# Attention scores in two slots of three PSUM banks instead of three slots of two

## The chip, the core and the metric

One core of a Trainium2 chip runs the whole program. The metric is the device time of one execution in microseconds (us), as the median of the runs. PE is the matrix engine (its weight loads have their own row, PEld), ACT the scalar engine, DVE the vector engine, POOL the GpSimd engine, SP the sync engine that issues most DMAs.

## The reference

```python
x = x + attn(layernorm(x))                       # x: 2 x 2048 x 512
x = x + ffn(layernorm(x))
# attn: q = 4 groups x 8 heads x 16, k and v = 8 heads x 16
scores = einsum('bsqhd,bthd->bqhst', qh, kh) * 16 ** -0.5
probs  = softmax(scores, axis=-1)                # 2 x 4 x 8 x 2048 x 2048
a_dot  = einsum('bqhst,bthd->bsqhd', probs, vh)
sigma_q = elu(q)
a_mem  = sigma_q @ memory / (sigma_q @ memory_norm)
out    = a_dot * (1 - w) + a_mem * w
# ffn: x quantised to fp8 and back, times the fp8 weight times its scale
```

The bulk is the softmax: 2 x 4 x 8 x 2048 x 2048 = 268 million exponentials.

## The kernel before, in words

After a prologue (projections, until about 168 us) the program works through 64 *heads* n = 0 to 63: eight chunks of 512 queries (n // 8), each with eight key heads (n % 8). A head has 64 *strips*; a strip is 128 keys x 512 queries of one query group, one PSUM bank. Four strips (the four query groups) over the same 128 keys make a key *tile*, and a head has 16 tiles. The last head (63) is done by code of its own (L1241, L1253), in units by query tile, and ends the program with the epilogue.

For a head, PE scores strips into PSUM, ACT takes their exponential into SBUF (`pool`), and PE weighs the values with them: matmuls of fp32 exponentials that accumulate over the whole head in PSUM banks 6 and 7. PE runs a step per *unit*. A unit is two strips (1024 columns): eight matmuls of 512 columns on eight 64x32 tiles of the array (L1038), then one exponential (L872). Weighing goes by key tile: 16 matmul instructions of 512 columns (L1154). Banks 0 to 5 are three slots of two banks, used in rotation by everything that PE hands over: a unit of scores waits (`slot_free`) until whoever read the slot three turns ago is done.

Not all strips go to ACT. DVE computes the exponential of the *late* strips of the next head by a polynomial: it takes them from PSUM (L1578), and a chain of six operations over 2048 columns (L1584 to L1598) leaves them in `late_probs`; PE weighs these at the next head's step 15 (`WEIGH_LATE_AT`). The last three operations of the chain (`chain_end`) are allowed only when PE has weighed the late strips that `late_probs` holds from the head before. Odd heads have 4 late strips; even ones have 6, the two more in a chain of 1024 columns of their own (`late_extra_strips`). So ACT has 30 units in an odd head and 29 in an even one.

Other things use slots as well: in each even head the memory term (`memory_products`, L1201, read by DVE in `add_memory`, L1718 and L1722), in odd heads a product of the ffn (L1188, read by L1711). Once the last weighing of a head is through (`pv_done`), DVE transposes banks 6 and 7 into SBUF (L1629, in `add_head`) and adds them up (L1632 to L1642); the first weighing of the following head waits for these transposes (`acc_read`). In even heads DVE also makes the moments of a ffn tile and rounds it to fp8 (L1660 to L1702). All these are in program order on DVE, written out in `head(n)` of its program.

Of the kernel before, what the change touches and what calls it, by code (L numbers as in the profile page):

```python
# [8 lines left out]
F32 = mybir.dt.float32  # L9
# [45 lines left out]
SLOTS = 3  # L55
SLOT_BANK = (0, 4, 2)
LATE_TILE = ST - 1
EXTRA_TILE = ST - 2
LATE = 2
RING = 3  # L60
# [4 lines left out]
LAST_RING = 2 * RING  # L65


LATE_AT = ((11, 12), (8, 9, 24))
MEMORY_AT = 7
WEIGHT_TURN_AT = 15  # L70
PRODUCT_AT = 1
LAST_PRODUCT_AT = 1
WEIGH_LATE_AT = 15
FIRST_WEIGH_AT = 5
WEIGHT_PAIR = KT - 1
# [3 lines left out]
def late_units(n):  # L79
    if not 0 < n < LAST_HEAD:  # L80
        return 0
    return LATE + (n % 2 == 0)


def exp_units(n):
    if n == LAST_HEAD:
        return LAST_UNITS
    return 2 * ST - late_units(n)


def late_at(n):
    return LATE_AT[n % 2][0:late_units(n + 1)]


def product_tile(n):
    tile = n // 2 - FIRST_PRODUCT_PAIR - 1
    return tile if (n % 2 == 1 or n == LAST_HEAD - 1) and tile >= 0 else None


def slot_turns(n):  # L100
    turns = []
    for a in range(exp_units(n)):
        if a in late_at(n):
            turns.append(("late", LATE_BASE[n + 1] + late_at(n).index(a)))
        if n == LAST_HEAD:
            if a == LAST_PRODUCT_AT:
                turns.append(("product", (NG - 1) * TPC - 1))
        elif a == PRODUCT_AT and product_tile(n) is not None:
            turns.append(("product", product_tile(n)))
        elif n % 2 == 0 and a == MEMORY_AT:  # L110
            turns.append(("memory", n // 2))
        elif n == 2 * WEIGHT_PAIR + 1 and a == WEIGHT_TURN_AT:
            turns.append(("weight", 0))
        turns.append(("exp", EXP_BASE[n] + a))
    return turns


LATE_BASE = [sum(late_units(m) for m in range(n)) for n in range(LAST_HEAD + 2)]
EXP_BASE = [sum(exp_units(m) for m in range(n)) for n in range(LAST_HEAD + 2)]
TURNS = [turn for n in range(LAST_HEAD + 1) for turn in slot_turns(n)]  # L120
TURN_NUMBER = {turn: i for i, turn in enumerate(TURNS)}


def slot_of(*turn):
    return TURN_NUMBER[turn] % SLOTS


def held_before(*turn):
    i = TURN_NUMBER[turn]
    return TURNS[i - SLOTS] if i >= SLOTS else None  # L130


def chains_before(n):
    return n - 1 + (n - 1) // 2


def late_weighed(n):
    return n * ST + LATE_BEFORE + 1


def last_place(v):
    return (v + 2 * probs_place(LAST_HEAD, 0)) % LAST_RING


def units_through(n, j):
    return min(2 * j + 2, exp_units(n))


def probs_place(n, j):
    return (j + (n > 0)) % RING  # L150


WEIGH_AT = {EXP_BASE[n] + max(units_through(n, j) - 1 + SLOTS, FIRST_WEIGH_AT): (n, j)
            for n in range(LAST_HEAD) for j in range((exp_units(n) + 1) // 2)}
LATE_BEFORE = sum(1 for at, (n, j) in WEIGH_AT.items() if n == 1 and at <= EXP_BASE[1] + WEIGH_LATE_AT)
# [43 lines left out]
def attention_ffn(nc, x, Wq, Wk, Wv, memory, memory_norm, memory_weight, weight, weight_scale, input_scale, out,  # L199
# [10 lines left out]
    with ExitStack() as ctx:  # L210
# [83 lines left out]
        late = sb("late", [P, 2 * 2 * LATE * CH], F32)  # L294
# [4 lines left out]
        late_extra = sb("late_extra", [P, 2 * CH], F32)  # L299
        xqT = sb("xqT", [P, KT, P], BF16)  # L300
        xq_now = sb("xq_now", [P, DM], BF16)
        probs = pool[:, 0:RING * QG * CH].rearrange("p (a b) -> p a b", a=RING)
        late_probs = pool[:, RING * QG * CH:(RING + 1) * QG * CH]
        late_x, late_z = (late[:, i * 2 * LATE * CH:(i + 1) * 2 * LATE * CH] for i in range(2))
        last_probs = pool[:, 0:RING * QG * CH].rearrange("p (a x q s) -> p a x q s", a=LAST_RING, x=2, q=QG)
# [15 lines left out]
        sc = [ps[:, i:i + 2, :] for i in SLOT_BANK]  # L321


# [91 lines left out]
        late_extra_ready = sem("late_extra_ready")  # L415
# [29 lines left out]
        def _(sp):  # L445
# [159 lines left out]
            def load_block(g, h, tile=None):  # L605
                n = g * HEADS + h
                par = h % 2
                sp.wait_ge(scores_ready, EXP_BASE[n - 1])
                copies = ROW_TILES
                if n == LAST_HEAD:  # L610
                    sp.wait_ge(last_cleared, 1)
                    copies = 1
                load_qk(n, g, h, par, operands_loaded[par], copies)
                load_guard(g, h, par, operands_loaded[par], copies)
                if tile is not None:
                    turn_tile(tile)
                sp.wait_ge(pv_done, (n - 1) * ST)
                load_v(g, h, par)
                if par == 0:
                    load_sigma(g * QG + h // 2)  # L620
# [144 lines left out]
        def _(act):  # L765
# [100 lines left out]
            for n in range(LAST_HEAD):  # L866
                for a in range(exp_units(n)):
                    unit = EXP_BASE[n] + a
                    j, half_u = divmod(a, 2)
                    held = probs[:, probs_place(n, j), :]  # L870
                    act.wait_ge(scores_ready, unit + 1)
                    act.activation(held[:, half_u * 2 * CH:half_u * 2 * CH + 2 * CH],  # L872
                                   sc[slot_of("exp", unit)].rearrange("p a b -> p (a b)"), ACT.Exp, bias=LIFT,
                                   scale=EXP_UNIT / SCORE_UNIT)\
                        .then_inc(probs_ready, 1)
                    if unit == LAST_V_AT:
                        copy_v(NG - 1, (NG - 1) % 2)
            for v in range(LAST_UNITS):
                unit = EXP_BASE[LAST_HEAD] + v
                act.wait_ge(scores_ready, unit + 1)  # L880
                act.activation(last_probs[:, last_place(v), :, :, :].rearrange("p x q s -> p (x q s)"),  # L881
                               sc[slot_of("exp", unit)].rearrange("p a b -> p (a b)"), ACT.Exp, bias=LIFT,
                               scale=EXP_UNIT / SCORE_UNIT)\
                    .then_inc(probs_ready, 1)
            def copy_turned(t, done, ks, bank):
# [17 lines left out]
        def _(pe):  # L903
# [129 lines left out]
            def unit_scores(dst, par, j, half_u):  # L1033
                for c in range(P // VW):
                    keys = j * P + c * VW
                    for x in range(ROW_TILES):
                        q = 2 * half_u + x
                        last = pe.matmul(dst[VW * c:VW * c + VW, x, :], k_st[RT * x:RT * x + AUG, par, keys:keys + VW],  # L1038
                                         q_st[RT * x:RT * x + AUG, par, q * CH:q * CH + CH], start=True, stop=True,
                                         tile_position=(RT * x, VW * c))  # L1040
                return last

            def score_early(u):
                unit_scores(sc[slot_of("exp", u)], 0, u // 2, u % 2).then_inc(early_scores, 1)
# [72 lines left out]
            def slot_free(*turn):  # L1117
                held = held_before(*turn)
                if held is None:
                    return  # L1120
                kind, number = held
                if kind == "exp":
                    pe.wait_ge(probs_ready, number + 1)
                elif kind == "late":
# [3 lines left out]
                elif kind == "weight":  # L1128
                    pe.wait_ge(wf_copied, 1)
                else:  # L1130
                    pe.wait_ge(y_ready, number + 1 + ONE_FREE)

            def scores(n, par, a):
                unit = EXP_BASE[n] + a
                if unit < EARLY_UNITS:
                    return
                slot_free("exp", unit)
                unit_scores(sc[slot_of("exp", unit)], par, a // 2, a % 2).then_inc(scores_ready, 1)

# [19 lines left out]
            def weigh_v(n, j):  # L1159
                if j == 0:  # L1160
# [657 lines left out]
```

## Time and profile before

| | |
|---|---|
| median of 3 runs | 1956.26 us (1954.72 to 1957.46) |
| the profiled execution | 1954.8 us, span 1952.7 us |
| busy | ACT 1848.2 us (95%), PE 1726.5 us (88%), DVE 1621.5 us (83%) |
| exponentials of heads 0 to 62 | 1861 instructions, 1724.6 us |

The busy figures are unions of the time in which an engine has an instruction in work. The granted TensorE clock is 1.0 over the whole span. The prologue and the epilogue are the same in both programs.

### The profile page before, as it was taken

What the parts mean: (1) busy time and instruction counts of PE and PEld (TensorE: products, weight loads), DVE (VectorE), ACT (ScalarE), POOL (GpSimd) and SP (SyncE); (2) the same over time, 40 slices, a digit from 0 to 9 for tenths busy, and PEclk for the clock granted to TensorE, in tenths of its full rate; (3) what the DMA queues carried; (4) which work ended last, traced back from release to release, by engine and by line L of the source; (5) the groups of instructions that cost most, each with busy time, mean ns of one, the idle gap of its engine ahead of it and who ended that gap; (6) DMA issues with size and microseconds to landing.
All of it is one profiled execution on the core that took longest, in us unless ns stands there. A gap on an engine that the chain in (4) does not pass through costs nothing.

```text
span 1952.7 us, 77800 instructions
## 1 busy us (share of the span) xinstructions
PE 1726.5 (88%) x35876; PEld 674.2 (35%) x35876; DVE 1621.5 (83%) x1893; ACT 1848.2 (95%) x2069; POOL 102.2 (5%) x150
## 2 busy tenths in 40 slices
PE   9999888888888888888888888888888888888888
PEld 7884222323223322333222232232223223332235
DVE  7675789888898889888888889888888898888975
ACT  5557999999999999999999999999999999999997
POOL 5541000000000000000000000000000000000000
PEclk9999999999999999999999999999999999999999
DMA  6564111121111221121111221121112211222111
GB/s 228 195 202 130 52 52 46 36 55 55 43 45 46 77 54 45 43 76 55 43 40 52 76 55 37 51 71 48 49 43 55 76 47 41 55 60 59 42 44 46
DMA packets 131183, 127.98 MB, mean 66 GB/s; under 512 B 30451, under 2 KB 106455, under 8 KB 130855
## 3 DMA queue, kind: packets, MB, share of 16 engines
q1 hardware_dynamic: 129847, 121.15, 21.1%
q8 instruction: 282, 4.62, 1.0%
q10 hardware_dynamic: 1008, 1.84, 0.3%
q14 instruction: 46, 0.38, 0.1%
HBM read 86.96 MB, written 32.24 MB: 61 GB/s over the span
## 4 chain that ended last, share of the span: by engine, by line
ACT 66%; PE 28%; issue 2%; SPq 1%; DMA 1%; DVE 1%; POOL 1%; PEld 0%; PEldq 0%; ACTq 0%; DVEq 0%; POOLq 0%
ACT pool L872 65%; PE ps L1154 10%; PE ps L1038 7%; PE ps L953 6%; PE ps L1201 2%; ACT pool L881 1%; PE ps L1188 1%; DMA q_st<-guard 1%; PE ps L926 1%; SPq L542 0%; DVE late L1578 0%; SPq L541 0%; DMA resid<-in_x 0%; POOL q_sq L730 0%; SPq L545 0%
## 5 line engine op out<-in xcount | busy, mean ns | idle before, releaser
L872 ACT ACTIVATE pool<-ps 128x1024 f32<-128x1024 f32 x1861 | 1724.6, 1115 | 16.5 <-PE ps L1038 9.5
L1154 PE MATMUL ps<-pool,v_st 64*32 64x512 f32 (+1 forms) x16128 | 1043.9, 583 | 22.7 <-issue 22.7
L1038 PE MATMUL ps<-q_st,k_st 51*32 51x512 f16 x16128 | 773.3, 381 | 181.4 <-ACT pool L872 173.1
L1038 PEld LDWEIGHTS ps<-q_st,k_st 51*32 51x32 f16 x16128 | 231.8, 90 | 1029.3 <-ACT pool L872 858.1
L1154 PEld LDWEIGHTS ps<-pool,v_st 64*32 64x32 f32 x16128 | 289.9, 106 | 132.7 <-issue 53.2
L1578 DVE TENSOR_SCALAR late<-ps 128x1024 int32<-128x1024 f32 x155 | 189.7, 1225 | 80.6 <-PE ps L1038 76.7
L1594 DVE SCALAR_TENSOR_TENSOR v_tiles<-late 128x2048 f32<-128x2048 f32 (+1 forms) x93 | 180.1, 1937 | 7.7
L1596 DVE SCALAR_TENSOR_TENSOR v_tiles<-v_tiles,late 128x2048 f32<-128x2048 f32 (+1 forms) x93 | 180.1, 1936 | 3.2
L1589 DVE SCALAR_TENSOR_TENSOR late<-late 128x2048 f32<-128x2048 f32 (+1 forms) x93 | 179.4, 1929 | 0.0
L1598 DVE SCALAR_TENSOR_TENSOR pool<-v_tiles,late 128x2048 f32<-128x2048 f32 x62 | 142.1, 2292 | 2.1
L1629 DVE STREAM_TRANSPOSE by_token<-ps 128x512 f32<-128x512 f32 x126 | 82.8, 695 | 63.0 <-PE ps L1154 63.0
L750 POOL TENSOR_TENSOR rstd<-var_eps,minus_half 128x1 f32<-128x1 f32 x32 | 18.3, 571 | 1716.9 <-DVE var_eps L1667 1716.9
L1587 DVE TENSOR_SCALAR late<-late 128x2048 int32<-128x2048 int32 (+1 forms) x93 | 97.6, 1050 | 3.2
L1584 DVE TENSOR_SCALAR late<-late 128x2048 int32<-128x2048 int32 (+1 forms) x93 | 97.6, 1050 | 3.2
L795 ACT ACTIVATE parts<-ps 128x512 f16<-128x512 f32 x40 | 23.9, 597 | 44.0 <-PE ps L953 44.0
L1477 DVE SCALAR_TENSOR_TENSOR y_out<-epos,ps 128x512 f32<-128x512 f32 x32 | 22.0, 688 | 46.4 <-ACT epos L804 46.3
L1718 DVE RECIPROCAL rnorm<-ps 128x4 f32<-128x4 f32 x32 | 5.8, 183 | 62.3 <-PE ps L1201 62.3
L953 PE MATMUL ps<-x_high,wqT 128*128 128x512 f32 x128 | 51.6, 403 | 0.0
L953 PE MATMUL ps<-x_high,wq_low 128*128 128x512 f32 x128 | 49.9, 390 | 0.0
L953 PE MATMUL ps<-x_low,wqT 128*128 128x512 f32 x128 | 46.2, 391 | 0.0
L1188 PE MATMUL ps<-wT_ffn,xqT 128*32 128x512 bf16 x448 | 29.3, 381 | 11.5 <-ACT pool L872 11.4
L1598 DVE SCALAR_TENSOR_TENSOR late_extra<-v_tiles,late 128x1024 f32<-128x1024 f32 x31 | 38.0, 1225 | 1.1
(172 smaller groups left out, 1042.0 us busy)
## 6 DMA issues: line engine op xcount, KB each, us to landing
v_st<-v_aug SPq DMA_DIRECT2D x64, 256.0 KB, 3.0
q_st<-q_aug SPq DMA_DIRECT2D x127, 128.0 KB
k_st<-k_aug SPq DMA_DIRECT2D x127, 128.0 KB
sigma_kept<-y_out SPq DMA_DIRECT2D x32, 256.0 KB, 2.0
q_aug<-parts SPq DMA_DIRECT2D x32, 256.0 KB, 2.8
wqT<-sigma_kept SPq DMA_DIRECT2D x32, 256.0 KB, 3.1
q_st<-q_aug SPq DMA_DIRECT2D x127, 64.0 KB
k_st<-k_aug SPq DMA_DIRECT2D x127, 64.0 KB
```

Of the source, the lines that this page charges most:

```text
L872: act.activation(held[:, half_u * 2 * CH:half_u * 2 * CH + 2 * CH], sc[slot_of("exp", unit)].rearrange("p a b -> p (a b)"), ACT.Exp, bias= ...
L953: return pe.matmul(bank(c, o), w, (x_high, x_low)[x_part][:, par, k, :], start=(k == 0 and p == 0), stop=(k == KT - 1 and p == len(PASSES) ...
L1038: last = pe.matmul(dst[VW * c:VW * c + VW, x, :], k_st[RT * x:RT * x + AUG, par, keys:keys + VW], q_st[RT * x:RT * x + AUG, par, q * CH:q ...
L1154: last = pe.matmul(acc[r][VW * c:VW * c + VW, :].rearrange("v (i s) -> v i s", s=VW)[:, places, :], v_st[rows, n % 2, j, :], by_place[rows ...
L1578: dve.tensor_scalar(late_x[:, place * 2 * CH:(place + 1) * 2 * CH].bitcast(I32), sc[slot_of("late", number)].rearrange("p a b -> p (a b)") ...
L1584: dve.tensor_scalar(part.bitcast(I32), fixed.bitcast(I32), MANTISSA, QUARTER, ALU.bitwise_and, ALU.bitwise_or).then_inc(late_step, 1)
L1587: dve.tensor_scalar(fixed.bitcast(I32), fixed.bitcast(I32), EXPONENT, ONE, ALU.bitwise_and, ALU.bitwise_xor).then_inc(late_step, 1)
L1589: dve.scalar_tensor_tensor(part, part, POWER[0], part, ALU.add, ALU.mult).then_inc(late_step, 1)
L1594: dve.scalar_tensor_tensor(grown, part, POWER[1], part, ALU.add, ALU.mult).then_inc(late_step, 1)
L1596: dve.scalar_tensor_tensor(grown, grown, POWER[2], part, ALU.add, ALU.mult).then_inc(late_step, 1)
L1598: return dve.scalar_tensor_tensor(dst, grown, POWER[3], power, ALU.add, ALU.mult)
L1629: last = dve.transpose(by_token[:, r, :, :, :].rearrange("p q t v -> p (q t v)"), acc[r])
```

## The change

A slot is now three banks, and there are two: banks 0 to 2 and 3 to 5. A *wide* unit is three strips (1536 columns) in one exponential, a *narrow* unit is two strips, and leaves the third bank of its slot (bank 2 or 3) free for an extra: one late strip, half of the memory term, a product, or half of the turned ffn weight. The order of units in a head is a list: an even head begins narrow, wide, narrow with the two halves of the memory term, and has its four late strips at units 10, 12, 14 and 16; an odd head has them at units 7, 9, 11 and 13. Every head has 22 units and 4 late strips, 6 narrow and 16 wide (head 0 has two narrow ones more); `late_extra_strips` is gone. Weighing goes by unit, so a unit that crosses a key tile is weighed in two pieces, and each late strip is a piece of its own.

```diff
-SLOTS = 3
-SLOT_BANK = (0, 4, 2)
+SLOTS = 2
+WIDE = 3
+PAIR_BANK = (0, 4)
+THIRD_BANK = (2, 3)
...
-LATE_AT = ((11, 12), (8, 9, 24))
-MEMORY_AT = 7
...
-WEIGH_LATE_AT = 15
-FIRST_WEIGH_AT = 5
...
+UNITS_OF_HEAD = (["2memory", "3", "2memory"] + ["3"] * 7 + ["2late", "3"] * 4 + ["3"] * 4,
+                 ["3", "3", "2product", "3", "2spare", "3", "3"] + ["2late", "3"] * 4 + ["3"] * 7)
+WEIGH_BEHIND = 2
+WEIGHED_LATER = ((0, 1, 2), (0, 1, 2, 3))
+WEIGH_LATE_AT = 17
...
+def weigh_at(u):
+    n = UNITS[u].head
+    return u + WEIGH_BEHIND + (u - EXP_BASE[n] in WEIGHED_LATER[n % 2])
...
+            def scores(u):
...
+                pe.wait_ge(probs_ready, u - SLOTS + 1)
+                if width < WIDE:
+                    pair_scores(u, n, strip).then_inc(scores_ready, 1)
+                    return
+                pair_first, third = ((0, 2), (1, 0))[u % SLOTS]
+                pair_scores(u, n, strip + pair_first)
+                third_free(u)
+                third_scores(u, n, strip + third).then_inc(scores_ready, 1)
...
+            def weigh_late(n, x):
                 pe.wait_ge(late_ready, n)
-                weigh(n, LATE_TILE, late_probs).then_inc(pv_done, 1)
+                last = weigh(n, LATE_TILE, late_probs[:, x * CH:x * CH + CH], x, 1)
+                if x == LATE - 1:
+                    last.then_inc(late_weighed, 1)
...
+                for u in range(EXP_BASE[n], EXP_BASE[n + 1]):
+                    scores(u)
+                    fill_extra_bank(u)
+                    for weighed in WEIGH_AT[u]:
+                        weigh_unit(weighed)
+                    x = u - EXP_BASE[n] - WEIGH_LATE_AT
+                    if n > 0 and 0 <= x < LATE:
+                        weigh_late(n, x)
...
+            def late_exponentials(n):
                 if n > 1:
                     dve.wait_ge(late_ready, n - 1)
-                    dve.wait_ge(late_extra_ready, (n - 1) // 2)
                 for x in range(LATE):
-                    take_late(n, x, x)
-                dve.wait_ge(late_taken, LATE_BASE[n] + LATE)
-                chain_begin(chains_before(n) * CHAIN_STEPS, LATE * 2 * CH)
...
+                    take_late((n - 1) * LATE + x)
+                dve.wait_ge(late_taken, n * LATE)
+                chain_begin((n - 1) * CHAIN_STEPS, LATE * CH)
...
-                    dve.wait_ge(pv_done, late_weighed(n - 1))
-                chain_end(chains_before(n) * CHAIN_STEPS, LATE * 2 * CH, late_probs).then_inc(late_ready, 1)
+                    dve.wait_ge(late_weighed, n - 1)
+                chain_end((n - 1) * CHAIN_STEPS, LATE * CH, late_probs).then_inc(late_ready, 1)
...
             def head(n):
                 g, h = divmod(n, HEADS)
-                if product_tile(n) is not None:
-                    ffn_out(*divmod(product_tile(n), TPC))
+                if n % 2 == 0:
+                    add_memory(n)
                 if n > 0:
-                    add_head(n - 1)
+                    take_sums(n - 1)
                 if n % 2 == 0:
-                    add_memory(g, h // 2)
+                    add_memory(n + 1)
+                if n > 0:
+                    add_sums(n - 1)
```

Three places in the order of instructions show what this does.

DVE, around the beginning of an even head of the second chunk or later. Before, the memory term follows the sums, and the late chains of the coming head are split in two:

```order
L1598 SCALAR_TENSOR_TENSOR late_extra<-v_tiles,late 128x1024 [waits late_step]
L1629 STREAM_TRANSPOSE by_token<-ps 128x512 [waits pv_done]
L1629 STREAM_TRANSPOSE by_token<-ps 128x512
L1632 TENSOR_TENSOR head_out<-by_token 128x272 [waits acc_read]
L1635 RECIPROCAL rden<-head_out 128x16 [waits halves_added]
L1637 TENSOR_TENSOR head_out<-head_out,rden 128x16x16 [waits rden_ready]
L1642 TENSOR_TENSOR resid<-resid,head_out 128x4x4x16 [waits head_out_ready]
L1718 RECIPROCAL rnorm<-ps 128x4 [waits am_ready]
L1722 SCALAR_TENSOR_TENSOR resid<-ps,rnorm,resid 128x128 [waits rnorm_ready]
L1722 SCALAR_TENSOR_TENSOR resid<-ps,rnorm,resid 128x128 x3
```

In the changed program, from the takes of the odd head's chain to the second half of the memory term:

```order
L1593 TENSOR_SCALAR late<-ps 128x512 [waits late_scores,late_ready]
L1593 TENSOR_SCALAR late<-ps 128x512 [waits late_scores] x3
L1598 TENSOR_SCALAR late<-late 128x2048 [waits late_taken]
L1601 TENSOR_SCALAR late<-late 128x2048 [waits late_step]
L1603 SCALAR_TENSOR_TENSOR late<-late 128x2048
L1608 SCALAR_TENSOR_TENSOR v_tiles<-late 128x2048 [waits late_step,late_weighed]
L1610 SCALAR_TENSOR_TENSOR v_tiles<-v_tiles,late 128x2048 [waits late_step]
L1612 SCALAR_TENSOR_TENSOR pool<-v_tiles,late 128x2048 [waits late_step]
L1724 RECIPROCAL rnorm<-ps 128x2 [waits am_ready]
L1728 SCALAR_TENSOR_TENSOR resid<-ps,rnorm,resid 128x128 [waits rnorm_ready]
L1728 SCALAR_TENSOR_TENSOR resid<-ps,rnorm,resid 128x128
L1631 STREAM_TRANSPOSE by_token<-ps 128x512 [waits pv_done]
```

The first half of the memory term now stands between the chain and the transposes, and the chain is followed by them directly.

PE, at the beginning of an even head. Before, steps 4 to 7 of such a head (L1038 scores a unit, L1154 weighs a tile, L1201 is the memory term):

```order
L1038 MATMUL ps<-q_st,k_st 32x512 [waits probs_ready]
L1038 MATMUL ps<-q_st,k_st 32x512 x7
L1154 MATMUL ps<-pool,v_st 32x512 [waits probs_ready,acc_read,values_loaded0]
L1154 MATMUL ps<-pool,v_st 32x512 x7
L1038 MATMUL ps<-q_st,k_st 32x512 [waits probs_ready]
L1038 MATMUL ps<-q_st,k_st 32x512 x7
L1154 MATMUL ps<-pool,v_st 32x512 [waits probs_ready]
L1154 MATMUL ps<-pool,v_st 32x512 x7
L1201 MATMUL ps<-mem_aug,wqT 32x129 [waits probs_ready,sigma_loaded]
L1201 MATMUL ps<-mem_aug,wqT 32x129 x15
```

In the changed program, units 2 to 4 of an even head (L1028 scores, L1153 weighs, L1200 is the memory term):

```order
L1028 MATMUL ps<-q_st,k_st 32x512 [waits probs_ready]
L1028 MATMUL ps<-q_st,k_st 32x512 x7
L1200 MATMUL ps<-mem_aug,wqT 32x129 [waits sigma_loaded,am_used]
L1200 MATMUL ps<-mem_aug,wqT 32x129 x7
L1028 MATMUL ps<-q_st,k_st 32x512 [waits probs_ready]
L1028 MATMUL ps<-q_st,k_st 32x512 x11
L1153 MATMUL ps<-pool,v_st 32x256 [waits probs_ready,acc_read,values_loaded0]
L1153 MATMUL ps<-pool,v_st 32x256 x7
L1028 MATMUL ps<-q_st,k_st 32x512 [waits probs_ready]
L1028 MATMUL ps<-q_st,k_st 32x512 x7
L1028 MATMUL ps<-q_st,k_st 32x512 [waits am_used]
L1028 MATMUL ps<-q_st,k_st 32x512 x3
```

The second half of the memory term waits, at unit 2, for DVE to have used the first (`am_used`), ahead of the scores of unit 3; the first weighing of the head stands at unit 3 instead of behind the scores of the sixth unit.

PE, the late strips. Before, all four are one weighing behind the scores of step 15:

```order
L1038 MATMUL ps<-q_st,k_st 32x512 [waits probs_ready]
L1038 MATMUL ps<-q_st,k_st 32x512 x7
L1154 MATMUL ps<-pool,v_st 32x512 [waits late_ready]
L1154 MATMUL ps<-pool,v_st 32x512 x7
L1038 MATMUL ps<-q_st,k_st 32x512 [waits probs_ready]
```

In the changed program each of units 17 to 20 has one of them (unit 20, the last, and the scores of unit 21):

```order
L1028 MATMUL ps<-q_st,k_st 32x512 [waits probs_ready]
L1028 MATMUL ps<-q_st,k_st 32x512 x11
L1153 MATMUL ps<-pool,v_st 32x384 [waits probs_ready]
L1153 MATMUL ps<-pool,v_st 32x384 x7
L1153 MATMUL ps<-pool,v_st 32x128 [waits late_ready]
L1153 MATMUL ps<-pool,v_st 32x128 x7
L1028 MATMUL ps<-q_st,k_st 32x512 [waits probs_ready]
```

The last late strip, whose weighing gives `late_weighed`, moved from the middle of the head to its last unit but one.

## Rows read from the trace of the kernel before

**Rows 1.** The page: busy time of each engine, share of the span, instructions
```profile
PE 1726.5 (88%) x35876; PEld 674.2 (35%) x35876; DVE 1621.5 (83%) x1893; ACT 1848.2 (95%) x2069; POOL 102.2 (5%) x150
```

**Rows 2.** Waits: who waited for whom, us in total, times, longest us
```profile
PEld ps L1038 <- ACT pool L872: 858.1, 1459, 1.4
...
DVE by_token L1629 <- PE ps L1154: 63.0, 62, 3.2
```

**Rows 3.** Timeline of ACT: start us, length us, what, [idle before <-releaser]
```profile
1033.31 1.02 ACT L872 ACTIVATE pool<-ps 128x1024 f32<-128x1024 f32 x1 [0.57 <-PE ps L1038]
...
1723.75 54.93 ACT L872 ACTIVATE pool<-ps 128x1024 f32<-128x1024 f32 x59 [0.17 <-PE ps L1038]
```

**Rows 4.** Groups by line: exponentials, first and last start, scores, a half-width ACTIVATE
```profile
L872 ACT ACTIVATE pool<-ps 128x1024 f32<-128x1024 f32 x1861 | 1724.6, 1115 | 16.5 <-PE ps L1038 9.5
L872 ACT ACTIVATE pool<-ps x1861: 1015/1111/1352, 168.6 to 1908.9; 128x1024 f32<-128x1024 f32 x187
L1038 PE MATMUL ps<-q_st,k_st 51*32 51x512 f16 x16128 | 773.3, 381 | 181.4 <-ACT pool L872 173.1
L795 ACT ACTIVATE parts<-ps 128x512 f16<-128x512 f32 x40 | 23.9, 597 | 44.0 <-PE ps L953 44.0
```

**Rows 5.** Timeline of PE: scores (L1038), weighing (L1154), memory term (L1201)
```profile
1669.71 0.62 PE L1038 MATMUL ps<-q_st,k_st 51*32 51x512 f16 x16
1670.15 1.04 PE L1154 MATMUL ps<-pool,v_st 64*32 64x512 f32 x16
1671.01 0.40 PE L1038 MATMUL ps<-q_st,k_st 51*32 51x512 f16 x8
...
1690.71 0.62 PE L1154 MATMUL ps<-pool,v_st 64*32 64x256 f32 x16
1691.14 0.62 PE L1154 MATMUL ps<-late_extra,v_st 64*32 64x256 f32 x16
...
1722.26 1.09 PE L1201 MATMUL ps<-mem_aug,wqT 128*32 128x129 f32 x32
1723.27 0.77 PE L1038 MATMUL ps<-q_st,k_st 51*32 51x512 f16 x16
```

**Rows 6.** Timeline of all engines: hand-overs from ACT to PE and back
```profile
1017.64 2.94 ACT L872 ACTIVATE pool<-ps 128x1024 f32<-128x1024 f32 x3
1018.80 0.11 PEld L1038 LDWEIGHTS ps<-q_st,k_st 51*32 51x32 f16 x8 [0.80 <-ACT pool L872]
1018.81 0.41 PE L1038 MATMUL ps<-q_st,k_st 51*32 51x512 f16 x8 [0.34 <-ACT pool L872]
...
1668.17 0.77 PE L1038 MATMUL ps<-q_st,k_st 51*32 51x512 f16 x16
1668.65 12.29 ACT L872 ACTIVATE pool<-ps 128x1024 f32<-128x1024 f32 x13 [0.17 <-PE ps L1038]
```

**Rows 7.** Timeline of PE in the last head: weighing in matmuls of 128 columns
```profile
1919.29 0.62 PE L1253 MATMUL ps<-pool,v_st 128*32 128x128 f32 x16
1919.72 0.61 PE L1241 MATMUL ps<-q_st,k_st 128*32 128x512 f16 x8
```

**Rows 8.** Timeline of DVE: memory term, a late chain, sums of a head
```profile
1668.31 0.18 DVE L1718 RECIPROCAL rnorm<-ps 128x4 f32<-128x4 f32 x1 [1.79 <-PE ps L1201]
1668.53 1.13 DVE L1722 SCALAR_TENSOR_TENSOR resid<-ps,rnorm,resid 128x128 f32<-128x128 f32 x4
...
1691.88 1.31 DVE L1629 STREAM_TRANSPOSE by_token<-ps 128x512 f32<-128x512 f32 x2 [1.44 <-PE ps L1154]
...
1698.69 1.23 DVE L1584 TENSOR_SCALAR late<-late 128x2048 int32<-128x2048 int32 x1
...
1703.48 2.29 DVE L1594 SCALAR_TENSOR_TENSOR v_tiles<-late 128x2048 f32<-128x2048 f32 x1
...
1708.14 2.29 DVE L1598 SCALAR_TENSOR_TENSOR pool<-v_tiles,late 128x2048 f32<-128x2048 f32 x1
```

**Rows 9.** Weight load of the first weighing after the transposes, all-engine timeline
```profile
1693.27 0.21 PEld L1154 LDWEIGHTS ps<-pool,v_st 64*32 64x32 f32 x16 [1.12 <-issue]
```

More of the change, by code:

```diff
@@ L1 @@
 import math
+from collections import namedtuple
 from contextlib import ExitStack
@@ L91, in late_at @@
-def late_at(n):
-    return LATE_AT[n % 2][0:late_units(n + 1)]
-def product_tile(n):
[L96 to L115, printed above, removed]
@@ L118 @@
[L118 to L134, printed above, removed]
@@ L137, in late_weighed @@
-def late_weighed(n):
-    return n * ST + LATE_BEFORE + 1
-def last_place(v):
[L142 to L155, printed above, removed]
+LAST_SLOTS = 3
@@ new lines, with extra_of @@
+LAST_RING = 6
+LAST_PRODUCT_AT = 2
+WEIGHT_HEAD = HEADS - 1
+FIRST_PRODUCT_PAIR = HEADS // 2
+UNITS_OF_HEAD = (["2memory", "3", "2memory"] + ["3"] * 7 + ["2late", "3"] * 4 + ["3"] * 4,
[3 more added lines that the diff above has]
+WEIGH_LATE_AT = 17
+Unit = namedtuple("Unit", "head strip width extra number")
+def product_tile(n):
+    return n // 2 - FIRST_PRODUCT_PAIR - 1
+def extra_of(n, name, i):
+    if name == "late" and n + 1 < LAST_HEAD:
+        return "late", n * LATE + i
+    if name == "memory":
+        return "memory", n + i
+    if name == "product" and product_tile(n) >= 0:
+        return "product", product_tile(n)
+    if n == WEIGHT_HEAD and name in ("product", "spare"):
+        return "weight", ("product", "spare").index(name)
+    if n == LAST_HEAD - 1 and (name, i) == ("late", 0):
+        return "product", product_tile(n)
+    return None, 0
@@ new lines, in units_of @@
+def units_of(n):
+    units, strip, names = [], 0, []
+    for form in ["2"] * EARLY_UNITS * (n == 0) + UNITS_OF_HEAD[n % 2]:
+        width, name = int(form[0]), form[1:]
+        units.append(Unit(n, strip, width, *extra_of(n, name, names.count(name))))
+        strip += width
+        names.append(name)
+    return units
+UNITS = [unit for n in range(LAST_HEAD) for unit in units_of(n)]
+EXP_BASE = [sum(unit.head < n for unit in UNITS) for n in range(LAST_HEAD + 1)]
+def weigh_at(u):
+    n = UNITS[u].head
+    return u + WEIGH_BEHIND + (u - EXP_BASE[n] in WEIGHED_LATER[n % 2])
@@ L1213, in turn_ffn_weight, with fill_extra_bank @@
                 last.then_inc(wf_turned, 1)
+            def fill_extra_bank(u):
+                kind, number = UNITS[u].extra, UNITS[u].number
+                if kind is not None:
+                    third_free(u)
+                if kind == "late":
+                    late_scored(u)
+                elif kind == "memory":
+                    memory_products(number)
+                elif kind == "product":
+                    ffn_product(number)
+                elif kind == "weight":
+                    turn_ffn_weight(number)
```

304 lines of the change are left out of this document (141 added, 163 removed).

## The prediction

> **What bounds the kernel now.** I read first the page's busy line [rows 1]: ACT is busy for 1848.2 of 1952.7 us, more than PE and DVE. The waits say who holds whom [rows 2]: PE's weight loads waited 858 us for L872, so PE is ahead and stands before full slots. The timeline of ACT [rows 3] shows how tight ACT is: 59 exponentials, those of an odd and an even head, run on for 54.93 us, then 0.17 us idle. So two heads cost 55.10 us. One exponential lasts 1.115 us [rows 4] and overlaps the next by 0.19: 58 spacings in 54.93 - 1.115 make 0.928 us each. One that starts after a wait lasts 1.02 [rows 3]. The stretch of these exponentials goes from 168.6 to 1908.9 + 1.02 [rows 4]: 1741.3 us, of which 1861 x 0.928 = 1727.0 are exponentials back to back and 14 are gaps.
>
> **The gain on ACT.** An ACTIVATE of 512 columns lasts 0.597 [rows 4], one of 1024 alone 1.02, so 512 columns more cost 0.425: a wide unit is spaced 1.353 and lasts 1.445 alone. Heads 0 to 62 had 3722 strips on ACT; now it is 3784 (64 + 62 x 60), in 380 narrow and 1008 wide units: 380 x 0.928 + 1008 x 1.353 = 1716.5 us. That is a gain of 10.5 on 1727.0: 473 fixed parts fewer, 62 strips more. "ScalarE: Activation LUTs" of the Trainium skill (section What ACT_TABLE_LOAD costs) has a higher fixed part: 186 ns, of which 93 overlap, plus 0.833 ns a column. By it the gain would be 17.6 us instead of 10.5; the spacing in the trace (0.928 where the page gives 0.946) is the measurement, and neither decides the case.
>
> **Can two slots feed ACT?** PE may score unit u when exponential u - 2 ends. ACT's end to PE's load is 0.05 (1017.64 + 1.115 to 1018.80), a pair lasts 0.41, four matmuls more 0.22 (sixteen in 0.62 to 0.63), PE's end to ACT's start 0.07 (1668.17 + 0.41 to 1668.65) [rows 5, 6]. A wide unit is ready 0.75 after its slot is free. Behind a narrow exponential the next would start 0.928 - 0.19 = 0.74 after it at best, and up to 0.83 costs nothing. Just enough; behind a wide one there are 0.4 to spare. PE's own work in a wide step: scores 0.44 (two groups, 1669.71 to 1670.15), weighing 0.86 x 3/4 = 0.65 (0.86 for four strips, 1670.15 to 1671.01) [rows 5], under 1.353. So the slots alone would let the gain through. I price them at nothing; if PE came 0.1 late behind each of the twelve narrow units of two heads, it would be 37 us.
>
> **Pieces.** A piece of one strip is 16 matmuls of 128 columns, a form not in the trace on these tiles. The pieces of 256 columns follow each other at 0.43, those of 512 at 0.86 [rows 5]: that goes with the columns, so 0.22 is the lower bound. The upper bound is 0.43, at which sixteen matmuls also go elsewhere, those of the last head with 128 columns on four tiles [rows 7]. I take 0.25: eight matmuls of scores, 0.381 long each on the mean [rows 4], are through in 0.41 [rows 6], so they start within 0.03, and sixteen such starts are far from filling 0.22.
>
> **What the change does to DVE, and so to PE.** This is the term that decides. I count from the end of a head's last exponential, before it negative. The `chain_end` of the next head's late strips waits for `late_weighed`, now given in step 20 of 22. That step begins when exponential 18 ends: -3 x 1.353 = -4.06. Then 0.05, scores 0.44, weighing of three strips 0.65, the late strip 0.25, its last matmuls 0.19 (0.62 long at a spacing of 0.43), hand-over to DVE 0.12 (1691.14 + 0.62 to 1691.88) [rows 5, 8]: -2.36. The first half of the chain takes 4.79 (1698.69 to 1703.48) [rows 8] and is done by then. The fourth take of an even head can start 0.75 after exponential 14 (-9.05), lasts some 0.69 and brings that half to its end at -2.8; in an odd head it is earlier. The last three operations take 6.95 (1703.48 to 1708.14 + 2.29). DVE is free at -2.36 + 6.95 = **+4.59**, in the next head, after every head. Before, it stood ready and waited for the sums, 62 times, 63 us in all [rows 2].
>
> *In an odd head* the transposes come then: 0.04 + 1.31 (5.94), PE's load 0.08 and matmul 0.01 later (6.03) [rows 8, 9]. PE has stood since step 3 at the weighing of unit 0, with unit 4's scores behind it. Weighing 0.65, scores of the narrow unit 0.41, hand-over 0.07: exponential 4 starts at 7.16 and ends at 8.18. Undisturbed it ends at 3 x 1.353 + 2 x 0.928 = 5.92. Loss 2.26. Then unit 1 is weighed in two pieces (0.22 + 0.43 + 0.25 after 6.68 make 7.58), unit 5 is scored by 8.21 and starts at 8.28: another 0.19. **Odd head 2.45.**
>
> *In an even head* the memory term comes first. Half of it costs DVE 0.18 + 0.04 + 0.57 (two of four operations in 1.13): 0.79 [rows 8], done at 5.42. PE has stood since step 2 at the second half, ahead of unit 3's scores. From 5.51 PE makes it: 0.43 for half the columns and 0.15 until scores flow, since the whole took 1.01 where its columns account for 0.86 (1722.26 to 1723.27) [rows 5]: 6.09. Scores 0.63, hand-over: exponential 3 starts at 6.79, ends at 8.24. The transposes end at 6.77, PE weighs unit 0 (6.86 to 7.29) and scores two strips of unit 4; the third waits for DVE's second half of the memory term, 7.60, and is there at 8.17. Exponential 4 ends at 9.62, undisturbed at 5.92. **Even head 3.70.** After both, PE catches up within some units, and the late takes find DVE free (sums, moments and rounding end at about 14.5, the first take is due at 15.8).
>
> Nothing of it is made up, since the next `late_weighed` hangs on exponential 18 of the delayed head. 31 pairs of heads: 31 x (2.45 + 3.70) = 190.7 us. DVE's work itself shrinks (no chain of 1024 columns, 8 takes of one strip for 5 of two), but its idle time stands where ACT runs, and its work where ACT waits.
>
> **Sum.** 1716.5 + 190.7 + 3 (gaps of the first heads, as before; the other 11 of the 14 sit at the old places of the memory term and go) = 1910.2 against 1741.3: +168.9. The profiled execution of 1954.8 becomes 2123.7; the median of the runs shown is 1.5 above it: **2125 us**. Chance 0.78.
>
> **Rivals.**
> *Small pieces are dear* (0.11). "TensorE: Matmul & The Clock Gate" of the Trainium skill (section Back-to-back issue gap) gives small matmuls a floor of about 25 ns from start to start; an estimate from that page is 0.40 us for sixteen. The bursts of scores, eight starts within 0.03 [rows 6], speak against such a floor on separate tiles, but only for eight. Worked out from rows, with 0.43 a piece: steps 17 to 20 need 1.5 to 1.75 us for 1.353, `late_weighed` comes 0.95 later, and some 0.18 is added at the head's start: 62 x 1.13 = 70 more, 2195 us.
> *The chain isn't held by `late_weighed`* (0.05), if PE got through the late strips sooner than counted. Then only even heads' chains spill over, to -2.8 + 6.95 = 4.2: 31 x 2.0 lost, +41: about 1998 us.
> *Faster* (0.03). The sums can't be taken before PE has weighed unit 21, at 0.05 + 0.44 + 0.65 + 0.19 + 0.12 = 1.45. If the chain were done by then, all would be hidden, and the gain is left: 1716.5 + 3 - 1741.3 = -21.8, 1934 us. From DVE free at about 2 it turns into a loss: the gain is 22 us over 62 heads, 0.35 each. For it speaks that DVE has less to do; against it that the six operations alone last 11.7 us from the fourth take, which is at -7.6 in an even head.
> *Something between* (0.03), around no change.
>
> **Numbers.** The likeliest case, with 0.3 us a head of error in hand-overs and backlog (19 us each way) and 0.22 to 0.3 for a piece, is 2100 to 2150. The range reaches to the dear pieces above: 2097 to 2192, about 8 in 10. No change means within 0.2%, about what a measurement of this kernel can tell. Faster 0.03, same 0.01, slower 0.96.
>
> **What the profile of the changed kernel would show.** ACT's timeline in runs: a gap of about 3.5 us (idle) after the third exponential of an even head, one of about 2.2 after the fourth of an odd one; two heads in 60.6 us instead of 55.1; L872's successor busy 1716 us or little more. PE's waits for DVE on `am_used` (resid) and on the transposes (by_token), each about 31 times 2 to 4 us. L1608 of DVE starting about 2.4 us before the head's end, after an idle wait for PE in odd heads of some 4 us. Sixteen matmuls of 128 columns spaced 0.25. Wrong would be: no such gaps (then the faster or the middle case), or ACT gaps of 0.1 to 0.3 all through a head (then the slots or the pieces are too tight).

## The result, and the profile after

The changed kernel takes 2181.89 us (median of 4 runs, 2171.43 to 2191.65) against 1956.19 before: a ratio of 1.115 (95% interval 1.110 to 1.121). Slower was forecast, at 2125 us in a range of 2097 to 2192. The profiled execution took 2186.5 us, its span is 2184.5.

The page of the changed kernel, its busy line and the group of the exponentials (busy, mean ns of one | idle before, releaser); they answer to [rows 1, 4]:

```profile
PE 1924.1 (88%) x55004; PEld 1250.2 (57%) x55012; DVE 1406.3 (64%) x1833; ACT 1848.3 (85%) x1596; POOL 106.9 (5%) x150
...
L865 ACT ACTIVATE pool<-ps 128x1536 f32<-128x1536 f32 (+1 forms) x1388 | 1724.8, 1399 | 247.2 <-PE ps L1028 241.7
```

DVE has 215 us less to do, and ACT as much as before. But ACT's exponentials had 16.5 us of idle time before them, and now 247.2. So the time is in waits for scores; who kept PE from them, the waits of the changed kernel say (us in total, times, longest); they answer to [rows 2]:

```profile
DVE late L1593 <- PE ps L1028: 488.5, 248, 5.9
PEld ps L1028 <- ACT pool L865: 350.8, 638, 1.2
ACT pool L865 <- PE ps L1028: 241.7, 130, 4.4
...
DVE v_tiles L1608 <- PE ps L1153: 149.3, 61, 5.1
PEld ps L1200 <- DVE resid L1728: 128.1, 31, 4.4
```

PE's second half of the memory term (L1200) waits for DVE's use of the first in each of the even heads 2 to 62. L1608, the first of the three held operations, waits for PE 61 times: that is `late_weighed`. The transposes (L1631) no longer wait for the sums, for which they waited 63 us before.

ACT's timeline of the changed kernel, over one even and one odd head; it answers to [rows 3], where 59 exponentials ran on without a wait:

```profile
1031.95 22.08 ACT L865 ACTIVATE pool<-ps 128x1024 f32<-128x1024 f32 x18 [0.23 <-PE ps L1028]
1058.18 2.80 ACT L865 ACTIVATE pool<-ps 128x1536 f32<-128x1536 f32 x2 [4.15 <-PE ps L1028]
1061.59 1.45 ACT L865 ACTIVATE pool<-ps 128x1536 f32<-128x1536 f32 x1 [0.61 <-PE ps L1028]
1063.23 24.84 ACT L865 ACTIVATE pool<-ps 128x1536 f32<-128x1536 f32 x20 [0.18 <-PE ps L1028]
1091.04 1.02 ACT L865 ACTIVATE pool<-ps 128x1024 f32<-128x1024 f32 x1 [2.96 <-PE ps L1028]
1092.80 24.57 ACT L865 ACTIVATE pool<-ps 128x1536 f32<-128x1536 f32 x20 [0.74 <-PE ps L1028]
```

The third exponential of the even head ends at 1031.95 + 22.08 = 1054.03, and 4.15 us of nothing follow; the fourth of the odd one ends at 1088.07, and 2.96 follow. In between ACT runs at its own pace. The next even gap ends at 1121.41: 63.2 us for two heads, where 55.1 was before and 60.6 was forecast.

The timeline of all engines of the changed kernel, across the end of the even head; it answers to [rows 8, 9] (DVE's rows, and as the last PE's weight load):

```profile
1080.76 2.29 DVE L1608 SCALAR_TENSOR_TENSOR v_tiles<-late 128x2048 f32<-128x2048 f32 x1 [0.37 <-PE ps L1153]
1083.09 2.29 DVE L1610 SCALAR_TENSOR_TENSOR v_tiles<-v_tiles,late 128x2048 f32<-128x2048 f32 x1
1085.42 2.29 DVE L1612 SCALAR_TENSOR_TENSOR pool<-v_tiles,late 128x2048 f32<-128x2048 f32 x1
1087.63 1.30 DVE L1631 STREAM_TRANSPOSE by_token<-ps 128x512 f32<-128x512 f32 x2
...
1089.00 0.26 PEld L1153 LDWEIGHTS ps<-pool,v_st 64*32 64x32 f32 x16 [3.01 <-issue]
```

The odd head's fourth exponential ended at 1088.07, which puts the end of the even head 4.99 earlier, at 1083.08. From there L1608 starts at -2.32 (worked out as -2.36), the chain ends at +4.63 (+4.59), and PE gets the banks at +5.92 (6.02). Up to here the walk of the prediction is met within 0.1 us. In the even head DVE comes 0.1 to 0.3 us earlier than worked out: counted from the head's beginning at 1050.82, the chain ends at +4.46 (1055.28; +4.59) and PE starts the second half of the memory term at +5.25 (1056.07; +5.51).

What follows is slower than worked out in both heads. The timeline of PE:

```profile
1056.07 1.09 PE L1200 MATMUL ps<-mem_aug,wqT 128*32 128x129 f32 x16 [3.57 <-DVE resid L1728]
1057.08 1.03 PE L1028 MATMUL ps<-q_st,k_st 51*32 51x512 f16 x9
...
1089.03 1.54 PE L1153 MATMUL ps<-pool,v_st 64*32 64x384 f32 x16 [2.54 <-issue]
1090.29 0.71 PE L1028 MATMUL ps<-q_st,k_st 51*32 51x512 f16 x8
```

Half of the memory term, priced at 0.58 until the next scores start, takes 1.01 (1056.07 to 1057.08), and the weighing of three strips, priced at 0.65, takes 1.26 (1089.03 to 1090.29). The windows of one microsecond of the changed kernel show why (the column after POOL is the granted clock of TensorE):

```profile
1052.00:1053.00 1.00, 0.49 (x16) 0.00 (x0) 0.97 (x2) 1.00 (x1) 0.00 (x0) 1.00 0.54 169
1053.00:1054.00 1.00, 0.00 (x0) 0.00 (x0) 1.00 (x1) 1.00 (x2) 0.00 (x0) 1.00 0.73 224
1054.00:1055.00 1.00, 0.00 (x0) 0.00 (x0) 1.00 (x1) 0.03 (x1) 0.00 (x0) 0.86 0.77 170
1055.00:1056.00 1.00, 0.00 (x0) 0.00 (x0) 0.96 (x5) 0.00 (x0) 0.00 (x0) 0.50 0.49 101
1056.00:1057.00 1.00, 0.94 (x16) 0.59 (x16) 1.00 (x3) 0.00 (x0) 0.00 (x0) 0.50 0.67 186
...
1060.00:1061.00 1.00, 1.00 (x40) 0.80 (x32) 0.89 (x4) 0.98 (x1) 0.11 (x1) 0.50 0.00 0
1061.00:1062.00 1.00, 1.00 (x45) 0.72 (x31) 0.49 (x2) 0.41 (x1) 0.61 (x1) 0.73 0.07 16
1062.00:1063.00 1.00, 1.00 (x54) 0.89 (x44) 0.93 (x3) 1.00 (x1) 0.00 (x0) 1.00 0.00 0
```

PE stood from 1052.5 to 1056.07, waiting for DVE. During that the granted clock went from 1.00 to 0.50, that is from 2.4 to 1.2 GHz, and it was back at 1.00 after PE had worked for some 5.5 us. So the work behind the wait, for which ACT stood, ran at the lower of the two levels. Behind PE's wait in the odd head it did too: the windows from 1089 to 1092 have 0.50. The mean granted clock of the run is 0.945; before it was 1.0.

### The profile page after: what moved, and what is told of

Same layout as the page of the kernel before. It is cut to its first block, busy times and chain, and to the rows that moved or that the text cites. A ratio compares the mean times of both kernels' runs of the same rounds, so it can differ in the third digit from the quotient of the medians.

```text
span 2184.5 us, 115411 instructions
## 1 busy us (share of the span) xinstructions
PE 1924.1 (88%) x55004; PEld 1250.2 (57%) x55012; DVE 1406.3 (64%) x1833; ACT 1848.3 (85%) x1596; POOL 106.9 (5%) x150
## 4 chain that ended last, share of the span: by engine, by line
ACT 50%; PE 33%; DVE 12%; issue 5%; POOL 0%; DMA 0%; PEld 0%; PEldq 0%; ACTq 0%; DVEq 0%; POOLq 0%
ACT pool L865 49%; PE ps L1153 15%; PE ps L1028 9%; PE ps L945 5%; DVE v_tiles L1608 3%; DVE v_tiles L1610 3%; DVE pool L1612 3%; PE ps L1200 1%; ACT pool L872 1%; PE ps L1187 1%; DVE resid L1728 1%; PE ps L918 1%; DMA resid<-in_x 0%; POOL q_sq L727 0%; PE ps L984 0%
## 5 line engine op out<-in xcount | busy, mean ns | idle before, releaser
L865 ACT ACTIVATE pool<-ps 128x1536 f32<-128x1536 f32 (+1 forms) x1388 | 1724.8, 1399 | 247.2 <-PE ps L1028 241.7
L1153 PE MATMUL ps<-pool,v_st 64*32 64x128 f32 (+2 forms) x35760 | 1457.5, 373 | 81.6 <-issue 81.5
L1153 PEld LDWEIGHTS ps<-pool,v_st 64*32 64x32 f32 x35760 | 913.0, 110 | 298.3 <-issue 151.5
L1028 PE MATMUL ps<-q_st,k_st 51*32 51x512 f16 x16128 | 961.4, 400 | 56.7 <-ACT pool L865 20.0
L1028 PEld LDWEIGHTS ps<-q_st,k_st 51*32 51x32 f16 x16128 | 285.6, 93 | 428.3 <-ACT pool L865 350.8
L1593 DVE TENSOR_SCALAR late<-ps 128x512 int32<-128x512 f32 x248 | 171.6, 692 | 488.5 <-PE ps L1028 488.5
L1608 DVE SCALAR_TENSOR_TENSOR v_tiles<-late 128x2048 f32<-128x2048 f32 x62 | 142.1, 2293 | 149.4 <-PE ps L1153 149.3
L1200 PE MATMUL ps<-mem_aug,wqT 128*32 128x129 f32 x1024 | 50.1, 323 | 109.4 <-DVE resid L1728 109.4
L1610 DVE SCALAR_TENSOR_TENSOR v_tiles<-v_tiles,late 128x2048 f32<-128x2048 f32 x62 | 142.1, 2292 | 2.1
L1603 DVE SCALAR_TENSOR_TENSOR late<-late 128x2048 f32<-128x2048 f32 x62 | 141.6, 2284 | 0.0
L1200 PEld LDWEIGHTS ps<-mem_aug,wqT 128*32 128x32 f32 x1024 | 28.3, 123 | 137.7 <-DVE resid L1728 128.1
L1631 DVE STREAM_TRANSPOSE by_token<-ps 128x512 f32<-128x512 f32 x126 | 82.2, 691 | 0.0
L1601 DVE TENSOR_SCALAR late<-late 128x2048 int32<-128x2048 int32 x62 | 76.1, 1227 | 2.1
L1598 DVE TENSOR_SCALAR late<-late 128x2048 int32<-128x2048 int32 x62 | 76.1, 1227 | 2.1
```

The lines of the kernel that those rows point to most:

```text
L865: act.activation(probs[:, u % HELD, 0:UNITS[u].width * CH], scored(u).rearrange("p a b -> p (a b)"), ACT.Exp, bias=LIFT, scale=EXP_UNIT / ...
L1028: return pe.matmul(ps[VW * c:VW * c + VW, bank, :], k_st[RT * r:RT * r + AUG, n % 2, keys:keys + VW], q_st[RT * r:RT * r + AUG, n % 2, q * ...
L1200: last = pe.matmul(am[VW * c:VW * c + VW, t * (KV + 1):(t + 1) * (KV + 1)], sigma_st[:, tokens:tokens + VW], mem_aug[:, :], start=True, st ...
L1593: dve.tensor_scalar(late_x[:, x * CH:x * CH + CH].bitcast(I32), extra_bank("late", number), -2.0 ** 23 / OCTAVE, LOWEST, ALU.mult, ALU.min ...
L1598: dve.tensor_scalar(part.bitcast(I32), fixed.bitcast(I32), MANTISSA, QUARTER, ALU.bitwise_and, ALU.bitwise_or).then_inc(late_step, 1)
L1603: dve.scalar_tensor_tensor(part, part, POWER[0], part, ALU.add, ALU.mult).then_inc(late_step, 1)
```

## The experiments

All times are medians of four runs, and the ratio is to the kernel before on the same chip (1956.7 us on one of the two used, 1956.6 on the other). Each edit is to the changed kernel; "..." stands for lines left out.

**The wait moved behind two operations.** Only the last of the three held operations writes `late_probs`, so the wait can stand there.

```diff
-            def chain_end(step, width, dst):
+            def chain_end(step, width, dst, weighed):
...
                 dve.wait_ge(late_step, step + 5)
+                if weighed > 0:
+                    dve.wait_ge(late_weighed, weighed)
                 return dve.scalar_tensor_tensor(dst, grown, POWER[3], power, ALU.add, ALU.mult)
...
-                else:
-                    dve.wait_ge(late_weighed, n - 1)
-                chain_end((n - 1) * CHAIN_STEPS, LATE * CH, late_probs).then_inc(late_ready, 1)
+                chain_end((n - 1) * CHAIN_STEPS, LATE * CH, late_probs, n - 1).then_inc(late_ready, 1)
```

> The wait for late_weighed stands before the last of the six operations of a late chain instead of before the last three; nothing else changes. Theory (DVE, held by late_weighed, reaches the memory term and the transposes 4.6 us into the next head): the chain of an odd head is now done at about the next head's beginning, that of an even head still at about 4.2 us after it (its own operations end there). The stall of even heads goes (some 5 us each, 31 times), that of odd heads shrinks by 0.4 us or, if PE's clock no longer drops there, to 2 us: 1992 to 2018 us. Rival (pieces of one strip or the two slots cost the time, DVE's stand is only seen beside it): within 15 us of 2182.

Measured: 2038.92 us, 1.041 (1.040 to 1.043), 143 us less. ACT's timeline of this kernel:

```profile
1017.32 1.02 ACT L865 ACTIVATE pool<-ps 128x1024 f32<-128x1024 f32 x1 [2.45 <-PE ps L1028]
1019.39 53.34 ACT L865 ACTIVATE pool<-ps 128x1536 f32<-128x1536 f32 x43 [1.04 <-PE ps L1028]
1075.01 1.02 ACT L865 ACTIVATE pool<-ps 128x1024 f32<-128x1024 f32 x1 [2.28 <-PE ps L1028]
```

43 exponentials in a row: the gap of even heads is gone, that of odd ones is left, as the theory has it. The place is shown. But 2039 lies above the 1992 to 2018 expected, and the gap of odd heads, 2.3 to 2.5 and then 1.0 to 1.1, is not the 2.05 in all. The granted clock of this run is 0.976.

**PE kept busy while it waits.** In both waits PE scores the next unit's pair again and again, into the banks where it will score it anyway.

```diff
                     scores(u)
+                    if n > 1 and u - EXP_BASE[n] == (2, 3)[n % 2]:
+                        pe.wait_ge(probs_ready, u)
+                        for i in range((12, 9)[n % 2]):
+                            pair_scores(u + 1, n, UNITS[u + 1].strip)
                     fill_extra_bank(u)
```

> While PE waits for DVE at the beginning of a head it scores the two strips of the next unit again and again (12 times in even heads, 9 in odd ones), and then goes on as before; the result is the same, and DVE and ACT have the same work. Theory (the 57 us that the prediction was short are PE at the lower clock after each wait of 3 to 4 us): granted clock 1.0 throughout, gaps of ACT as worked out in the prediction (two heads in 60.6 us), 2125 us, give or take 10. Rival (the clock costs nothing, the 57 us are hand-overs and backlog): 2182 or up to 20 more, for the added matmuls.

Measured: 2114.92 us, 1.080 (1.079 to 1.082): 67 us less by 5136 matmuls more. The granted clock is 0.998. Two heads in ACT's timeline of this kernel:

```profile
1023.78 4.13 ACT L865 ACTIVATE pool<-ps 128x1536 f32<-128x1536 f32 x3 [3.27 <-PE ps L1028]
...
1055.13 25.66 ACT L865 ACTIVATE pool<-ps 128x1024 f32<-128x1024 f32 x21 [2.10 <-PE ps L1028]
1084.06 28.87 ACT L865 ACTIVATE pool<-ps 128x1536 f32<-128x1536 f32 x23 [3.27 <-PE ps L1028]
```

Two heads take 60.3 us (1023.78 to 1084.06; 60.6 forecast), the main gaps are 3.27 and 2.10 (worked out: 3.58 from 3.21 to 6.79, and 2.17 from 4.99 to 7.16). At the high clock the prediction's walk holds within about 0.3 us a head, though the whole came out 10 us under its 2125.

**Both together, in odd heads.** The moved wait as above, and eight pairs of scores repeated in the wait that is left.

```diff
+                    if n % 2 == 1 and u - EXP_BASE[n] == 3:
+                        pe.wait_ge(probs_ready, u)
+                        for i in range(8):
+                            pair_scores(u + 1, n, UNITS[u + 1].strip)
```

> The wait for late_weighed before the last operation of the chain, and in odd heads PE scores the next unit eight times more while it waits for the transposes. Theory (what was above the forecast with the moved wait alone, 2039 against 1992 to 2018 us, is the lower clock after PE's wait in odd heads): granted clock 1.0, 31 stalls of 2.05 us are left, 1998 us, give or take 8. Rival: 2039.

Measured: 1998.20 us, 1.021 (1.019 to 1.023), granted clock 1.0. The 41 us to the run with the moved wait alone went with the clock: 0.976 there, 1.0 here, from repeated scores that add work to PE.

**One operation more in the held part.**

```diff
-CHAIN_STEPS = 5
+CHAIN_STEPS = 6
...
+                for again in range(2):
                     dve.scalar_tensor_tensor(grown, part, POWER[1], part, ALU.add, ALU.mult).then_inc(late_step, 1)
-                dve.wait_ge(late_step, step + 4)
+                    dve.wait_ge(late_step, step + 4 + again)
...
-                dve.wait_ge(late_step, step + 5)
+                dve.wait_ge(late_step, step + 6)
```

> One operation of 2048 columns (2.33 us with its gap) more in the held part of each chain; the result is the same. Theory (the held part of the chain is on the path in every head): 62 x 2.33 = 145 us more, 2327 us, up to 2350 if PE's clock stays low for longer. Rival (DVE has idle time, 36% of the span, and takes the operation out of it): 2182.

Measured: 2364.54 us, 1.209 (1.207 to 1.211): 182.7 us more, 2.95 for each of the 62 chains, though DVE was idle for over a third of the span. That is more than the 2.33 of the operation and above the upper end expected. The profiled execution ran for about 425 us at the lower clock (mean 0.91) against 240 in the changed kernel (0.945), which goes the right way; that it makes up the other 38 us wasn't tested. The rival, DVE hiding it in its idle time, is out.

**Two operations less.**

```diff
+                few = slice(0, 64)
-                dve.scalar_tensor_tensor(grown, part, POWER[1], part, ALU.add, ALU.mult).then_inc(late_step, 1)
+                dve.scalar_tensor_tensor(grown[:, few], part[:, few], POWER[1], part[:, few], ALU.add, ALU.mult).then_inc(late_step, 1)
                 dve.wait_ge(late_step, step + 4)
-                dve.scalar_tensor_tensor(grown, grown, POWER[2], part, ALU.add, ALU.mult).then_inc(late_step, 1)
+                dve.scalar_tensor_tensor(grown[:, few], grown[:, few], POWER[2], part[:, few], ALU.add, ALU.mult).then_inc(late_step, 1)
```

> Two of the three held operations of each chain work on 64 columns instead of 2048, so the polynomial of the late strips is left incomplete. Theory: DVE is free at 0.2 us after the end of an odd head and before the end of an even one, ahead of what it waits for then (the sums, at 1.45); all stalls go and what is left is the price of the exponentials: 1934 us, up to 1945. Rival (two slots too few behind narrow units, or pieces too dear): 1971 us or more, with ACT gaps of 0.1 us and more all through a head.

Measured: 1933.84 us, 0.989 (0.987 to 0.990). ACT's timeline of this kernel:

```profile
1145.82 380.54 ACT L865 ACTIVATE pool<-ps 128x1536 f32<-128x1536 f32 x309 [0.28 <-PE ps L1028]
```

The page of this kernel, its group of exponentials (busy, mean ns of one | idle before, releaser):

```profile
L865 ACT ACTIVATE pool<-ps 128x1536 f32<-128x1536 f32 (+1 forms) x1388 | 1707.9, 1421 | 10.9 <-PE ps L1028 9.3
```

309 exponentials, 14 heads, without a wait that the view shows (it leaves out idle time under 0.15 us). So two slots do feed ACT, nearly everywhere also behind narrow units, and the pieces of one strip fit into PE's time. A wide exponential is worth a little more than was worked out: with 84 narrow ones at 0.928, the 224 spacings of wide ones in this row come to 1.344 us each, where 1.353 was taken.

**Early strips alone.** Late strips of even heads at units 6 to 12, and the seven roundings between the takes; the wait and the late weighing as in the changed kernel.

```diff
-UNITS_OF_HEAD = (["2memory", "3", "2memory"] + ["3"] * 7 + ["2late", "3"] * 4 + ["3"] * 4,
+UNITS_OF_HEAD = (["2memory", "3", "2memory"] + ["3"] * 3 + ["2late", "3"] * 4 + ["3"] * 8,
...
                 for x in range(LATE):
                     take_late((n - 1) * LATE + x)
+                    for _ in range(3):
+                        next(between, None)
...
-                        round_to_float8((g - 1) * TPC + h // 2, xq_now[:, :])
+                        between = round_to_float8((g - 1) * TPC + h // 2, xq_now[:, :])
```

(`round_to_float8` hands over after each of its operations.)

> Late strips of even heads at units 6 to 12 and the rounding between the takes, but late strips are weighed at units 17 to 20 and the wait for late_weighed stands before the last three operations, as in the changed kernel. Theory (the last three operations begin when unit 20 is through, whenever the strips were taken): 2182 us, give or take 15. Rival (the late position of the takes is what makes the chain spill over): both heads as with the moved wait or better, 2039 us or less.

Measured: 2172.60 us, 1.109 (1.106 to 1.112). The takes of an even head come some 6 us earlier and its chain isn't done earlier: DVE's timeline of this kernel has it waiting for the late weighing instead, 5.95 us where it was 0.37.

```profile
1008.24 2.29 DVE L1608 SCALAR_TENSOR_TENSOR v_tiles<-late 128x2048 f32<-128x2048 f32 x1 [5.95 <-PE ps L1153]
```

**The chain kept in its head.** Early strips, the moved wait, and late strips weighed at units 14 to 17.

```diff
-WEIGH_LATE_AT = 17
+WEIGH_LATE_AT = 14
```

> A version meant to keep the whole chain inside its head: even heads have their late strips at units 6, 8, 10 and 12 instead of 10 to 16, the seven operations of rounding to fp8 stand between the four takes, late strips are weighed at units 14 to 17, and the wait for late_weighed stands before the last operation of the chain. Theory: DVE is free at -1.3 us in even heads and 0.1 us in odd ones, and no head begins with a stall: 1934 us, up to 1945, faster than the kernel before. Rival (the rounding between the takes delays them and so PE, whose next late strip waits for the take; or PE has too little room where late strips, narrow units and late weighings follow each other): 1950 us or more.

Measured: 1942.78 us (1941.25 to 1945.41), 0.993 (0.991 to 0.995): a version that is faster than the kernel before, by 0.7%, and 239 us faster than the changed one. DVE's timeline of this kernel, at the end of an even head:

```profile
1019.14 2.29 DVE L1614 SCALAR_TENSOR_TENSOR pool<-v_tiles,late 128x2048 f32<-128x2048 f32 x1
1024.03 1.31 DVE L1633 STREAM_TRANSPOSE by_token<-ps 128x512 f32<-128x512 f32 x2 [2.59 <-PE ps L1153]
```

DVE waits for the sums again, as it did before the change. It is 9 us over the 1934 that the shortened chain reached; its exponentials had 18.4 us of idle time before them against 10.9 there. Which of the single gaps is whose wasn't followed up.

## Why the prediction was right, and where it was short

- **The gain on ACT** (10.5 us, all in all 22 with the gaps): right in the sum, and the sum was lucky. With the stalls gone, the run with the shortened chain took 1933.8 us; 1934 was worked out. But its exponentials were busy for 1707.9 us against 1724.6 before, 16.7 less where 10.5 was worked out (wide ones are spaced 1.344, not 1.353), and their idle time was 10.9 against 16.5, 5.6 less where 11 was expected. The two errors nearly cancel.
- **Two slots feed ACT, priced at nothing**: right within a few us. In the same run 25 of the even heads' second exponentials, each behind a narrow one, were up to 0.8 us late, 3.6 us in all; the rest of the 10.9 are single gaps. The sum had left 3 for all of them.
- **Pieces of one strip at 0.25 us**: step 20 came out as summed, but not by its terms. PE's timeline of the changed kernel:

```profile
1077.09 0.92 PE L1153 MATMUL ps<-pool,v_st 64*32 64x128 f32 x43
...
1079.15 0.47 PE L1028 MATMUL ps<-q_st,k_st 51*32 51x512 f16 x8
1079.38 0.48 PE L1153 MATMUL ps<-pool,v_st 64*32 64x384 f32 x1
...
1080.50 0.41 PE L1028 MATMUL ps<-q_st,k_st 51*32 51x512 f16 x8
```

  By the trace's single records, weighing begins 0.23 after the step's scores, not 0.44, and the three strips take 0.65. The sixteen matmuls of the late strip then start from 1080.03 to 1080.37, 23 ns apart, and are through at 1080.64, which is -2.44; -2.48 was worked out (late strip and last matmuls). So the piece was longer than 0.25 here, and the shorter scores made up for it. The next scores, at 1080.50, waited for the end of exponential 19 at 1080.44, so their start prices nothing. The rival of dear pieces is out all the same: `late_weighed` came on time and not 0.95 later, and with the shortened chain ACT ran on. The floor of about 25 ns for small matmuls ("TensorE: Matmul & The Clock Gate" of the Trainium skill, section Back-to-back issue gap) isn't what this trace shows on separate tiles of the array. The 43 matmuls of the first row follow each other at 15.5 ns ((0.92 - 0.27) / 42, one lasting 0.27). Why they are 23 ns apart in one place and 15.5 in the other wasn't followed up.
- **The held chain, DVE free at +4.59, PE standing at unit 2 and unit 3**: right, at +4.63 and +4.46 in the trace; shown by the moved wait (143 us less), by one operation more (183 more) and by two fewer (248 less).
- **The losses of 2.45 us in an odd head and 3.70 in an even one**: this is the term that was mis-sized. It took PE's durations from a trace in which TensorE's clock never fell. In the two heads shown PE stands for 2.5 and 3.6 us at the beginning, and the granted clock falls to 0.50 for the work on which ACT waits. In the two heads shown exponential 6 of the even head ends at 13.86 (1063.23 + 1.45 from 1050.82) where 8.62 would be undisturbed: 5.24 lost, not 3.70. In the odd head exponential 5 ends at 11.17 (1092.80 + 1.45 from 1083.08) where 7.27 would be: 3.90, not 2.45. Over the 30 pairs from head 2 to head 62 the mean is 62.54 us ((2116.32 - 239.99) / 30, the starts behind the even gaps), where 54.43 undisturbed and 6.15 lost make 60.58. In 31 pairs that is 61 of the 63 us by which the profiled execution (2186.5) lies above the 2123.7 worked out for it. That it is the clock, the run with PE kept busy shows: 60.35 a pair, and 67 us less in all.
- **What would show it wrong** had only DVE, the slots and the pieces. A wait of 3 us on PE was seen coming, and its price on the clock wasn't asked for, although the sum rested on PE's speed right behind it. The 57 us between 2125 and 2182 were a quarter of the 226 that the change cost.

## What to carry to other kernels

An engine at 64% busy can be the bound: what counts is where its long run of dependent operations begins and what is queued behind it. Here moving one wait past the two operations that didn't need it was worth 143 of 226 us, and moving the work earlier without it 9, less than the 20 by which the changed kernel's own runs scatter. And when a change makes PE stand for microseconds, the work behind the wait is to be priced at the lower clock too.

## What the runs showed of the hardware that was not expected

The fall of the clock is not the same after like waits. In the changed kernel PE stood twice for 2.54 us before the first weighing of an odd head. Behind the one at 1089.03 sixteen matmuls of 384 columns took 1.54 us, behind the one at 1151.38 they took 0.88. PE's timeline of the changed kernel:

```profile
1089.03 1.54 PE L1153 MATMUL ps<-pool,v_st 64*32 64x384 f32 x16 [2.54 <-issue]
...
1151.38 0.88 PE L1153 MATMUL ps<-pool,v_st 64*32 64x384 f32 x16 [2.54 <-issue]
```

The windows of one microsecond of the same kernel show that the granted clock (the column after POOL) was 1.00 throughout in the second case:

```profile
1151.00:1152.00 1.00, 0.62 (x16) 0.39 (x24) 0.93 (x3) 0.00 (x0) 0.00 (x0) 1.00 0.00 0
1152.00:1153.00 1.00, 1.00 (x56) 0.86 (x45) 0.93 (x4) 0.47 (x1) 0.00 (x0) 1.00 0.00 0
```

In this trace the clock fell behind all 31 beginnings of even heads from 2 on, and behind 20 of the 31 of odd heads. This may also be why this kernel's times scatter by 20 us (2171 to 2192), while those of the kernel before lie within 8 over all runs (1952.6 to 1959.7); that wasn't tested. What decides between the two cases stays open.
